# A fused two-block transformer kernel: routing weights spread by DMA instead of by matmul, and half of the state additions on GpSimd

## What is computed

```python
h = layernorm(x) * (1 + ca) + sa
x = x + ga * softmax_attention(h)               # block 0: 16 heads of depth 8
h = layernorm(x) * (1 + cb) + sb
x = x + gb * experts0(h)                        # 64 routed experts of 88, top 8, and 2 x 88 shared rows
h = layernorm(x) * (1 + ca') + sa'
x = x + ga' * delta_rule_attention(h)           # block 1: a scan over 16 positions
h = layernorm(x) * (1 + cb') + sb'
x = x + gb' * experts1(h)                       # 8 experts of 512, top 2, and a null expert
```

```python
rw = route(x)                                   # [tokens, 64], zero but for 8 experts of a token
routed = sum_e rw[:, e] * (silu(x @ Wg[e].T) * (x @ Wu[e].T)) @ Wd[e].T
```

```python
v_bar = W @ k_i
W = W + outer(b_i * (v_i - v_bar), k_i)         # the state addition
y_i = W @ q_i
```

## Time and profile before

| | us |
|---|---|
| median of 3 runs | 1984.51 (1984.31 to 1989.08) |
| the profiled execution | 1989.54 |
| its span (first to last instruction) | 1987.7 |
| TensorE busy | 1782.0 (90%) |
| VectorE busy | 1425.5 (72%) |
| ScalarE busy | 809.7 (41%) |
| Pool busy | 677.8 (34%) |
| DMA: moved over the span | 157.68 MB, 79 GB/s |

### The profile page before, as it was taken

How to read it: one execution, slowest core, us unless ns; L and a number is a source line. 1 busy time by engine, 2 the same in 40 slices (tenths; PEclk the granted TensorE clock), 3 DMA queues, 4 the chain that set the end, 5 groups by cost and what they waited for, 6 DMA issues and landing times. The chain is left out here.

```text
span 1987.7 us, 25546 instructions
## 1 busy us (share of the span) xinstructions
PE 1782.0 (90%) x7668; PEld 1062.7 (53%) x7668; DVE 1425.5 (72%) x2688; ACT 809.7 (41%) x1501; POOL 677.8 (34%) x610
## 2 busy tenths in 40 slices
PE   2888898652999999999899899998998999999999
PEld 1455555351666656656566565565664455555555
DVE  5777777378666786986979969779699487444444
ACT  1466667532333324334343233342434443443333
POOL 2011111100000681945828638368194275000000
PEclk9989889855999999999999999999999999999999
DMA  7544444010223353333333333333330000000000
GB/s 267 151 134 111 120 119 115 23 51 13 104 106 111 101 178 94 99 90 97 89 95 98 87 95 95 90 100 85 95 101 11 1 6 6 6 6 5 6 5 5
DMA packets 101065, 157.68 MB, mean 79 GB/s; under 512 B 11077, under 2 KB 49310, under 8 KB 97785
## 3 DMA queue, kind: packets, MB, share of 16 engines
q1 hardware_dynamic: 97351, 154.61, 26.1%
q10 hardware_dynamic: 1586, 1.30, 0.2%
q0 software_dynamic: 2048, 0.79, 0.2%
HBM read 123.23 MB, written 33.42 MB: 79 GB/s over the span
## 5 line engine op out<-in xcount | busy, mean ns | idle before, releaser
L1296 PE MATMUL psum<-e_hhi,e_ring 128*128 128x512 f32 x704 | 478.2, 679 | 37.5 <-DVE e_hm L1737 26.2
L1551 ACT ACTIVATE e_gu<-psum 128x512 f32<-128x512 f32 (+1 forms) x368 | 219.1, 597 | 627.8 <-PE psum L1298 510.5
L1305 PE MATMUL psum<-e_hm,w_d 128*128 128x512 f32 (+1 forms) x736 | 378.6, 597 | 1.1 <-DVE e_hm L1733 1.1
L1733 DVE TENSOR_TENSOR e_gu<-psum,e_gu 128x512 f32<-128x512 f32 x352 | 240.9, 684 | 174.2 <-PE psum L1335 158.6
L1801 POOL TENSOR_TENSOR e_prod<-e_state,e_phi 128x512 f32<-128x512 f32 x256 | 355.3, 1424 | 5.5 <-DVE e_y L1608 3.2
L1769 DVE TENSOR_TENSOR e_hm<-psum,e_gu 128x512 f32<-128x512 f32 x256 | 175.2, 689 | 203.7 <-ACT e_gu L1576 152.0
L1297 PE MATMUL psum<-e_hhi,e_ring 128*128 128x512 f32 x704 | 281.2, 399 | 0.0
L1298 PE MATMUL psum<-e_hlo,e_ring 128*128 128x512 f32 x704 | 280.5, 399 | 0.0
L1415 PE MATMUL psum<-e_hm,w_gu 128*128 128x512 f32 x512 | 264.0, 601 | 3.2 <-DVE w_d L1751 2.6
L1576 ACT ACTIVATE e_gu<-psum 128x512 f32<-128x512 f32 x256 | 152.4, 597 | 279.0 <-PE psum L1298 264.8
L1737 DVE TENSOR_TENSOR e_hm<-psum,e_gu 128x512 f32<-128x512 f32 x352 | 243.5, 692 | 12.1
(11 more groups left out here) (237 smaller groups left out, 2404.7 us busy)
## 6 DMA issues: line engine op xcount, KB each, us to landing
e_ring<-w_split SPq DMA_DIRECT2D x308, 256.0 KB, 2.6
qk_parts<-at_part SPq DMA_DIRECT2D x96, 192.0 KB, 2.9
w_split<-e_ring SPq DMA_DIRECT2D x44, 256.0 KB, 2.0
at_qs<-qk_parts SPq DMA_DIRECT2D x16, 576.0 KB
at_ks<-qk_parts SPq DMA_DIRECT2D x16, 576.0 KB
w_gu<-in_w SPq DMA_DIRECT2D x2, 2048.0 KB, 10.4
sel_buf_r<-w_split SPq DMA_DIRECT2D x14, 256.0 KB, 2.6
w_gu<-in_wg SPq DMA_DIRECT2D x1, 2904.0 KB
```

The source lines that it names most:

```text
L1296: pe.matmul(out, w_hi, x_hi, start=first, stop=False)
L1305: mm = pe.matmul(ps[:, ACC, :], weights_at(T, WD + P * j, P)[0:rows(j), :], hm[0:rows(j), slot(j), :], start=(j == 0), stop=(j == HT - 1))
L1551: a(act_g[0:r, j % 2, :], ps[0:r, GB[j % 2], :], ACT.Silu).then_inc(silu_done, 1)
L1733: ins = v.tensor_tensor(product, ps[0:r, UB[j % 2], :], act_g[0:r, j % 2, :], ALU.mult)
```

## The change

1. **Routing weights.** The three bf16 parts, the one-hot matrix `sel` and its load, and the spreading matmul are gone. TensorE turns the fp32 weights directly (32 transposes), ScalarE and VectorE keep alternate chunks in fp32, and SyncE stores them to a DRAM tensor `rw_dram` [64, 4096], eight DMAs. In `experts` SyncE loads for each routed tile a buffer `rb` [128, 512] (four slots) by two or three DMAs, one for each expert that owns rows of the tile, each of which reads one DRAM row of 2 KB into all of that expert's partitions.
2. **Order of the products.** VectorE first multiplies the up projection by `rb` and writes that into the PSUM bank `RB`; the second product multiplies it by silu into `hm`. The wait for silu now stands before the second product, and a wait for `rb_in` before the first.
3. **State additions.** VectorE keeps those of z = 0 (tiles 29 and 43). Those of z = 1 go to Pool, in four pieces, between the outer products and the query products.

```diff
+            for c in range(CHUNKS):
+                sp.wait_ge(tr_kept[c % 2], c // 2 + 1)
+                sp.dma_start(cols(T["rw_dram"], c), cols(rw_fm, c)[0:EXPERTS]).then_inc(rw_out, 16)
+            sp.wait_ge(rw_out, 16 * CHUNKS)
...
+            for c in range(CHUNKS):
+                pe.wait_ge(weighted, 1 + c // (CHUNKS // 2))
+                if c >= 4:
+                    pe.wait_ge(tr_kept[c % 2], c // 2 - 1)
+                for t in range(CT):
+                    mm = pe.transpose(ps[0:EXPERTS, 2 + c % 4, t * P:(t + 1) * P], w1[:, (CT * c + t) * EXPERTS:(CT * c + t + 1) * EXPERTS],
+                                      T["ident"][:])
+                mm.then_inc(tr_done, 1)
...
+RB_SLOTS = 4
+def owners(j):
+    rows = range(P * j, P * (j + 1))
+    return [(max(HIDDEN * e, rows[0]) - rows[0], min(HIDDEN * (e + 1), rows[-1] + 1) - rows[0], e)
+            for e in range(rows[0] // HIDDEN, rows[-1] // HIDDEN + 1)]
...
-        ADD_SLOT = {29: (0, 0), 31: (0, 1), 43: (1, 0), 45: (1, 1)}
+        ADD_SLOT = {29: 0, 43: 1}
...
+            def load_rb(c, j):
+                if j >= ROUTED_TILES:
+                    return
+                if c > 0 or j >= RB_SLOTS:
+                    sp.wait_ge(gu_done, ROUTED_TILES * c + j - RB_SLOTS + 1)
+                s = j % RB_SLOTS
+                for first, last, e in owners(j):
+                    sp.dma_start(rb[first:last, s, :], T["rw_dram"][e:e + 1, c * CHUNK:(c + 1) * CHUNK].broadcast_to([last - first, CHUNK]))\
+                        .then_inc(rb_in[s], 16)
...
                 sp.dma_start(split[j], w_slots[slot_of(j)].bitcast(F32)).then_inc(split_out[slot_of(j)], 16)
+                load_rb(0, j)
...
                     sp.dma_start(w_slots[slot_of(j)].bitcast(F32), split[j]).then_inc(split_in[slot_of(j)], 16)
+                    load_rb(c, j)
...
                 mm = three(ps[0:r, UB[j % 2], :], w_slot(j, 0, 1), w_slot(j, 1, 1), h_hi[:], h_lo[:])
-                if j < ROUTED_TILES:
-                    mm = pe.matmul(ps[:, RB[j % 2], :], sel[0:PARTS * EHALF, j % HALF_TILES, :],
-                                   rw[0:PARTS * EHALF, j // HALF_TILES, ds(c * CHUNK, CHUNK)], start=True, stop=True)
                 mm.then_inc(ur_done, 1)
...
-                    dve.wait_ge(silu_done, g + 1)
                     dve.wait_ge(ur_done, g + 1)
-                    product = gu[0:r, j % 2, :] if j < ROUTED_TILES else hm[0:r, slot(j), :]
-                    ins = v.tensor_tensor(product, ps[0:r, UB[j % 2], :], act_g[0:r, j % 2, :], ALU.mult)
                     if j < ROUTED_TILES:
-                        ins.then_inc(gu_done, 1)
+                        s = j % RB_SLOTS
+                        dve.wait_ge(rb_in[s], 16 * rb_loads(s, ROUTED_TILES) * c + 16 * rb_loads(s, j + 1))
+                        v.tensor_tensor(ps[:, RB[j % 2], :], ps[0:r, UB[j % 2], :], rb[:, s, :], ALU.mult).then_inc(gu_done, 1)
+                        dve.wait_ge(silu_done, g + 1)
                         dve.wait_ge(gu_done, ROUTED_TILES * c + j + 1)
-                        v.tensor_tensor(hm[:, slot(j), :], ps[:, RB[j % 2], :], gu[:, j % 2, :], ALU.mult).then_inc(hm_done, 1)
+                        v.tensor_tensor(hm[:, slot(j), :], ps[:, RB[j % 2], :], act_g[:, j % 2, :], ALU.mult).then_inc(hm_done, 1)
...
                         pieces(prod[:, z], wide(heads(uz)), tall(key), ALU.mult).then_inc(pool_step, 1)
+                    pool.wait_ge(pool_step, at + OUTER[1])
+                    pieces(state[:, 1], state[:, 1], prod[:, 1], ALU.add).then_inc(added1, 1)
                     for z in range(LT):
                         t = LT * s + z
-                        pool.wait_ge(added, CT * m + t + 1)
+                        pool.wait_ge(added if z == 0 else added1, CB * m + s + 1)
                         pieces(prod[:, z], state[:, z], tall(phi[:, 0, t]), ALU.mult).then_inc(pool_step, 1)
```

More of the change, by code:

```diff
@@ L878, in _ @@
             run(pe, step_)
-            pe.wait_ge(cut, 1)
-            pe.wait_ge(T["ffn0_loaded"], 16 * FFN0_LOADS)
-            def turn(c, k):
-                if k >= 2:
-                    for g in range(2):
-                        pe.wait_ge(tr_kept[g], c - 1)
-                for g in range(2):
-                    for t in range(CT):
-                        mm = pe.matmul(ps[0:PARTS * EHALF, 2 + 2 * (k % 2) + g, t * P:(t + 1) * P],
-                                       parts[:, ds(CT * c + t, 1), g, :, :].rearrange("p o i e -> p (o i e)"), T["ident_bf"][:],
-                                       start=True, stop=True)
-                mm.then_inc(tr_done, 1)
-            turn(0, 0)
-            turn(1, 1)
-            pe.wait_ge(cut, 2)
-            with pe.Fori(1, CHUNKS // 2) as i:
-                turn(2 * i, 2)
-                turn(2 * i + 1, 3)
+            for c in range(CHUNKS):
[5 more added lines that the diff above has]
+                                      T["ident"][:])
+                mm.then_inc(tr_done, 1)
         @block.scalar
@@ L921, in _ @@
                 nc.scalar.activation(lg[:, over(u)], lg[:, over(u)], ACT.Sigmoid).then_inc(scored, 1)
-            for u in range(2):
-                act.wait_ge(weighted, u + 1)
-                nc.scalar.activation(part(0, u), half(w1, u), ACT.Copy).then_inc(upper_cut, 1)
-            for u in range(2):
-                act.wait_ge(rest_ready, u + 1)
-                nc.scalar.activation(part(1, u), half(w0, u), ACT.Copy).then_inc(upper_cut, 1)
-            def keep(c, k):
-                act.wait_ge(tr_done, c + 1)
-                nc.scalar.activation(T["rw"][0:PARTS * EHALF, 0, ds(c * CHUNK, CHUNK)], ps[0:PARTS * EHALF, 2 + 2 * (k % 2), :], ACT.Copy)\
-                    .then_inc(tr_kept[0], 1)
-            with act.Fori(0, CHUNKS // 2) as i:
-                keep(2 * i, 0)
-                keep(2 * i + 1, 1)
+            for c in range(0, CHUNKS, 2):
+                act.wait_ge(tr_done, c + 1)
+                nc.scalar.activation(cols(rw_fm, c)[0:EXPERTS], ps[0:EXPERTS, 2 + c % 4, :], ACT.Copy).then_inc(tr_kept[0], 1)
         @block.vector
@@ L1057, with rb_loads @@
 W_SLOTS = 5
+RB_SLOTS = 4
[3 more added lines that the diff above has]
+            for e in range(rows[0] // HIDDEN, rows[-1] // HIDDEN + 1)]
+def rb_loads(slot, j):
+    return sum(len(owners(i)) for i in range(j) if i % RB_SLOTS == slot)
 def slot_of(j):
@@ L1190, in experts @@
         split_in = [sem(f"split_in{s}") for s in range(W_SLOTS)]
+        rb_in = [sem(f"rb_in{s}") for s in range(RB_SLOTS)]
         w1h_done, w1l_done = sem("w1h_done"), sem("w1l_done")
@@ L1686, in jobs @@
                     if j in ADD_SLOT:
-                        s, z = ADD_SLOT[j]
-                        dve.wait_ge(pool_step, pool_at(m, s, OUTER[z]))
-                        v.tensor_tensor(state[:, z], state[:, z], prod[:, z], ALU.add).then_inc(added, 1)
+                        s = ADD_SLOT[j]
+                        dve.wait_ge(pool_step, pool_at(m, s, OUTER[0]))
+                        v.tensor_tensor(state[:, 0], state[:, 0], prod[:, 0], ALU.add).then_inc(added, 1)
                     if j in Y_SLOT:
@@ L1922, in layout @@
     a["wo"] = i["L1_attn_Wo"]
-    owner = (np.arange(HALF_TILES * P) // HIDDEN).reshape(HALF_TILES, P)
-    one_hot = (owner[None] == np.arange(EHALF)[:, None, None])
-    a["sel"] = f(np.tile(one_hot, (PARTS, 1, 1)).astype(bf16))
     a["wr"] = i["L1_ffn_router_w"]
```

40 lines of the change are left out of this document (11 added, 29 removed).

## The result

In the runs made for the comparison the kernel before took 1988.53 us in the median (1984.31 to 1989.72, 5 runs) and the changed one **1972.77** (1970.14 to 1979.78, 5 runs): ratio 0.9934, 95% interval 0.9910 to 0.9959, so 16 us by the medians and some 13 by the ratio. The forecast was a gain of 44 us, and 1968 us at the upper end of its range. The profiled execution is the longest of the five (1979.78 us).

The account below looks back on a forecast made before the run. TensorE was taken to pace each chunk's first half, VectorE from tile 24, with Pool just in time. Gains of 6.4 + 10.2 + 4.3 + 22.2 + 1.3 = 44.4 us took the median from 1984.5 to 1940, range 1930 to 1968.

Parts of the forecast that it names:

- Routing before the chunks: Stage ahead of chunk 0: 32 fp32 transposes replace bf16 parts and transposes; gain 6.4 us, bounds 3 and 7.
- TensorE's step: Where TensorE paces: a tile falls from 2.50 to 2.27 us without the spreading matmul.
- Chunk 0: First chunk, TensorE busy 117.95 of 120 us: 44 spreading matmuls at 0.233 us go, gain 10.2.
- Cost 0 while the TensorE or VectorE pace covers it: Broadcast-row loads on SP's queue: at the dearest 1.9 of each 2.27 us per tile, so no cost.
- Chunk 1: Chunk without router: Pool's chain starts 4.7 us earlier, y sum 2.7 earlier, 1.6 more behind it; gain 4.3.
- Chunks 2 to 7: Six chunks: u starts 5.7 us earlier, Pool's addition takes 4.1, 2.1 of hold goes; gain 3.7 each, 22.2 together.
- the wait at tile 33: First y sum: VectorE waits about 3 us for Pool's query products, eating what giving up its addition gains.
- The order of products: VectorE's two products per tile: silu's wait moves to the second, which can only help; PSUM destination costs 0.
- Into the second experts' stage: After the last chunk: the addition no longer holds the first product; gain 1.3 us.
- (a): Half the gain: dearer PSUM destination, Pool pieces at 5.0, routing gain only 3; 1959 us, chance 0.17.
- (b): Slower: the queue becomes the bound through dearer broadcast loads; 1991 to 2012 us, chance 0.13.
- (c): VectorE paces everything, so moved spreading has no effect; only routing, entry and chunk 0 gain 18 us: 1967, chance 0.10.

Follow-up runs that it names:

- e8: Against e1: in chunk 0 the broadcast rows of tile j+1 are asked for before the store of tile j's split weights; 1952.84 us.
- e3: Against the changed kernel: broadcast rows of tiles 0 to 3 loaded once in chunk 0 and reused for all tiles and chunks (wrong output); 1960.05 us.
- e2: Against the kernel before: only the state addition of every second position moved to Pool, spreading matmul kept; 2004.88 us.
- e5: Against the changed kernel: Pool's addition put between the query products of the two positions, third and fourth y sums one tile later; 1953.46 us.
- e11: Against the changed kernel with the edits of e5 and e8: VectorE's wait for silu back at the first product; 1945.84 us.
- e1: Against the changed kernel: routing part alone, all four state additions back on VectorE at tiles 29, 31, 43 and 45; 1957.62 us.

## Why the prediction was wrong

The sign was right; the size was not, and the time lies outside the range. By its own steps:

**Routing before the chunks, forecast 6.4: held, at 7.4.** From the end of the weightings to chunk 0's `h_low` it was 477.05 to 495.25, 18.2 us, and is 480.77 to 491.57, 10.8. The table above shows only 3.7 because the stages ahead ran 3.7 longer in that execution; across the profiles with the new routing code the start moves between 480.0 and 491.6. The 32 transposes took 5.10 us, not 7.3.

**TensorE's step, 2.27 per tile: held.** Down projections in chunk 4 stand at 1051.20, 1053.44, 1055.68, so 2.24 apart. From the sum at tile 2 to the one at tile 24 a chunk of the loop gained 4.7 us.

**Chunk 0, forecast 10.2: 7.0.** "Cost 0 while the TensorE or VectorE pace covers it" failed. I had given a row 8.4 us from its request; the request hung on SP's order behind a store that waits for VectorE's split, and the weight stores and loads landed in 3.5 to 3.8 instead of 2.0 to 2.6. The share of rows and weights together was priced, but not what it does to each landing, nor what SP waits for ahead of a row. `e8` gives 4.7 us back in this chunk. The Trainium skill ("DMA: Bandwidth & Descriptors", why a DMA increments its semaphore by 16) has it that the number of engines must divide the rows of a load; no view here shows which engines carried the rows. At 0.95 us for each load, my dearest reading, the share in the loop would have doubled to 0.68; it was 0.62. But it is no even share: in chunk 1, six stretches of 15 us from its start show 0.81, 0.90, 0.66, 0.64, 0.89 and 0.83, so there the queue was at times as full as I had feared (1.9 of 2.27 us is 0.84).

**Chunk 1, forecast -4.3: +3.4.** The step that failed is the "-4.7", Pool's chain starting earlier. The first product waits 3.82 us for TensorE (2.02 before, and 2.01 in `e3` without rows), and at tile 7 the chunk is 3.3 late where `e3` is 1.8 early. So Pool's key products start at +62.2, 1.3 later than before (+60.9); in `e3` they start at +57.1, 3.8 earlier. With the addition at 5.0 and 2.1 of hold less, the y sum comes 4.2 later than before, and VectorE waits 6.8 us for it. In `e3` the chunk is 116.9.

**Chunks 2 to 7, forecast -3.7 each: 0, but -0.7 in chunk 7.** Three terms failed, read in chunk 4. (1) The start: the addition at tile 45 "lay mostly under the restart of TensorE" was true, but I concluded that the first tiles would move up. They did not: the first product came at +4.5 as before, and the residual of tile 1 at +6.8 instead of +5.9. Where the addition had stood there is now the gap of 3.83 us for which the profile shows nothing (in chunks 3 and 7 the sum at tile 2 also waits 2.05 and 1.66 for Pool, in chunks 4 to 6 it does not). Of the 5.7 for u 2.0 were lost by then. (2) Pool's four pieces took 5.00 us, my upper bound, not 4.1; they are as dear as state times phi, the row I had put at the far end. The Trainium skill ("GPSIMD Engine Reference", section 3.1) gives 4.5 for one addition of 2048 fp32 elements; the trace has 5.00 for it in four pieces, and that decides. (3) "Behind that VectorE's work runs without gaps, as before, to tile 45" failed by 1.0: TensorE, with less to do, idles longer behind the router cut and returns at the low clock for longer. 3.7 - 2.0 - 0.9 - 1.0 is -0.2, and the chunk is 0.2 longer.

**The step behind all this** is the one that treated the wait at tile 33 as the price of the addition: "What VectorE gains by giving up the addition is thus eaten by this wait". The wait was priced at 3 and came out at 4.05, and `e2` shows that the move is no even trade but costs 1.9 to 4.4 us in each of chunks 3 to 6. I put Pool's chain end to end and never asked whether the addition of the second position had to stand ahead of the queries of the first. It had not, and `e5` puts that order at 19 us, of the 29 by which the median gain fell short. The forecast did price this order; what it had wrong are the three terms above, and the order is what one could have changed.

**The order of products, "can only help": wrong in the written-out chunks.** There the second product's extra wait makes a pair 1.40 instead of 1.32 us. `e11` shows the cause, and that it is worth no more than the noise of the total.

**Into the second experts' stage, forecast 1.3:** the rest after the last `h_low` is 2.4 shorter; I cannot split that.

**The rivals.** (a) had one of its three causes: Pool at 5.0 came. A dearer PSUM destination did not (693 against 684 ns, and pairs of 1.33 us in the loop against 1.32), and a routing gain of only 3 did not (7.4). (b), the queue as the bound in every tile, did not come. (c), VectorE pacing everything, gave the nearest number (1967), but by luck: `e1` and `e5` show that chunks of the loop do get some 3 us shorter once Pool's addition is out of the way.

## What to carry to other kernels

When work is moved to an engine that works in series and just in time, decide its place in that series by who waits for what comes behind it; here the same instructions cost 19 us more in one place than in another. A load that stands in SP's order behind other work is asked for only when the latest thing ahead of it is done, so write out for each one what SP waits for first, not only how long it takes to land. And an engine that is relieved can idle longer at the next bottleneck (3.81 instead of 3.45 us here); where it is TensorE, look at the granted clock after that idle time before counting the gain.
